# Two layers of a graph transformer on one core: one product per 128 edges for the edge counts, half of the target patterns made as steps by ScalarE, edges loaded first

## The reference, cut to what matters

```
xn  = layernorm(x)
x   = x + gnn(xn, edges) + linear_attention(xn)
x   = x + mixture_of_experts(layernorm(x))        # 16 experts, top 2
```

```
h   = xn @ W + b
adj = zeros(256, 256); adj[src, dst] = 1; adj[dst, src] = 1; adj += eye
adj = adj / row_sum
out = d0 * h + d1 * adj h + d2 * adj^2 h + d3 * adj^3 h ; relu
```

## Time and profile before

| | |
|---|---|
| three runs | 239.66 us median, 238.54 to 239.84 |
| the profiled execution | 238.44 us, its span 236.7 us |
| mean granted clock of TensorE | 0.986 |
| PE busy | 221.0 us, 93% of the span |
| DVE, ACT, POOL busy | 139.3, 51.4, 21.2 us |
| `idle_turns` (133 products recorded in all) | 18.0 us |
| count products, 128 | 14.6 us recorded, 14.0 us of the chain |
| one-hot patterns, 128 | 27.0 us |

### The profile page before, as it was taken

How to read it: one execution, slowest core, us unless ns; L and a number is a source line. 1 busy time by engine, 2 the same in 40 slices (tenths; PEclk the granted TensorE clock), 3 DMA queues, 4 the chain that set the end, 5 groups by cost and what they waited for, 6 DMA issues and landing times.

```text
span 236.7 us, 2953 instructions
## 1 busy us (share of the span) xinstructions
PE 221.0 (93%) x1065; PEld 148.9 (63%) x1065; DVE 139.3 (59%) x432; ACT 51.4 (22%) x118; POOL 21.2 (9%) x36
## 2 busy tenths in 40 slices
PE   0699999999999989999999999999988999989994
PEld 0584647598569866985455668549674454648851
DVE  2796689995488813324062726979771649534312
ACT  2103021132202011211001116971082412014200
POOL 2940100000010200000005000000020001010000
PEclk9999999999999589999999999999999999999999
DMA  6998894001999000004604000000000000000002
GB/s 156 332 404 319 324 415 161 0 3 39 384 408 405 8 0 0 3 0 138 217 33 147 0 1 1 0 3 0 0 0 3 0 0 0 1 0 3 0 0 89
DMA packets 8669, 23.65 MB, mean 100 GB/s; under 512 B 2376, under 2 KB 2376, under 8 KB 8400
## 3 DMA queue, kind: packets, MB, share of 16 engines
q1 hardware_dynamic: 8656, 23.48, 26.9%
HBM read 22.95 MB, written 0.52 MB: 99 GB/s over the span
## 4 chain that ended last, share of the span: by engine, by line
PE 88%; DVE 6%; DMA 1%; POOL 1%; issue 1%; ACT 1%; SPq 0%; DVEq 0%
PE bank L1102 16%; PE bank L1076 13%; PE bank L1194 9%; PE bank L1206 9%; PE bank L1113 7%; PE bank L1151 6%; PE bank L1255 6%; PE bank L1245 3%; PE bank L1157 3%; PE bank L1158 2%; PE bank L1142 2%; PE bank L1090 2%; PE bank L1293 1%; DVE xT L586 1%; DMA xa<-in_x 1%; PE bank L1294 1%
## 5 line engine op out<-in xcount | busy, mean ns | idle before, releaser
L1102 PE MATMUL bank<-raw,xT 128*128 128x512 f32 x88 | 39.1, 594 | 0.0
L773 DVE TENSOR_SCALAR ring<-iota_bf,edges 128x256 bf16<-128x256 bf16 x128 | 27.0, 300 | 5.4 <-PE bank L1255 5.3
L1102 PEld LDWEIGHTS bank<-raw,xT 128*128 128x128 f32 x88 | 16.4, 190 | 18.9 <-issue 18.7
L303 POOL TENSOR_TENSOR rstd<-veps,minus_half 128x1 f32<-128x1 f32 x14 | 8.7, 632 | 170.8 <-DVE veps L573 89.1
L1194 PE MATMUL bank<-xT,raw 128*128 128x256 f32 x96 | 22.7, 386 | 0.0
L1206 PE MATMUL bank<-raw,ring 128*128 128x512 f32 x48 | 21.0, 594 | 0.0
L1194 PEld LDWEIGHTS bank<-xT,raw 128*128 128x128 f32 x96 | 17.6, 190 | 3.1 <-issue 0.9
L1245 PE MATMUL bank<-iota_bf 128*128 128x256 bf16 x133 | 18.0, 295 | 0.3 <-ACT wa L336 0.3
L1113 PE MATMUL bank<-xT,raw 128*128 128x256 f32 x64 | 16.2, 411 | 0.8 <-DVE xT L586 0.8
L1245 PEld LDWEIGHTS bank<-iota_bf 128*128 128x128 bf16 x133 | 14.0, 106 | 4.2 <-issue 1.1
L1206 PEld LDWEIGHTS bank<-raw,ring 128*128 128x128 f32 x48 | 9.0, 190 | 10.9 <-issue 10.5
(11 more groups left out here) (241 smaller groups left out, 323.6 us busy)
## 6 DMA issues: line engine op xcount, KB each, us to landing
raw<-in_up SPq DMA_DIRECT2D x6, 512.0 KB, 9.2
raw<-in_down SPq DMA_DIRECT2D x6, 512.0 KB, 11.0
raw<-in_k SPq DMA_DIRECT2D x4, 512.0 KB, 9.0
raw<-in_q SPq DMA_DIRECT2D x4, 512.0 KB, 9.8
raw<-in_v SPq DMA_DIRECT2D x4, 512.0 KB, 11.3
raw<-in_out SPq DMA_DIRECT2D x4, 512.0 KB, 8.8
raw<-in_gat SPq DMA_DIRECT2D x4, 512.0 KB, 6.7
raw<-in_gnn SPq DMA_DIRECT2D x2, 512.0 KB, 10.2
```

The costliest lines, as they stand in the source:

```text
L303: nc.gpsimd.tensor_tensor(rstd[:, t:t + 1], veps[:, t:t + 1], minus_half[:, t:t + 1], ALU.pow)\
L773: ins = V.tensor_scalar(onehot[:, j % RING, a, :], iota_bf[:, :], edges[:, a, j:j + 1], None, ALU.is_equal)
L1102: ins = mm(bank[banks[t]][:, :], xT_at(c, t), w.at(c), start=c == 0, stop=c == C - 1)
```

## The change

- **Counts.** A source is split in its number modulo 128 and a digit that says whether it is 128 or more. The pattern of sources has 128 columns and holds the value 1, or -4096 where the digit is set (`radix`). One product per `j` of 128 weights by 256 columns gives both halves of the sources in one number: count of the low half minus 4096 times count of the high half. There are 64 products in place of 128.
- **Targets.** For even `j` DVE writes the one-hot pattern of the targets as before. For odd `j` ACT writes `Sign(iota - dst + 0.5)`, a step that is -1 below the target and +1 from it on (line 414). Even `j` are summed in bank 2, odd ones in bank 3; DVE takes the differences of neighbours of half the sum of bank 3, adds up, converts to integers, shifts by 12 bits, and takes the two halves apart: ten instructions more (lines 820 to 837). The result is laid out as `countT`, and PE transposes it into `count`.
- **Pieces.** The ring has 20 slots of 384 values; the counts stand in pieces of 20, 20 and 24, all ahead of gnn0. The gnn0 product is cut in its two tiles, the second behind the context product.
- **Start.** `src` and `dst` are loaded ahead of `x`. DVE's work on `iota` and on the edges stands ahead of the statistics of `x`. PE does 20 `idle_turns` before the first transposes.
- **After.** Parts 0 and 1 of the small products stand behind step 2, parts 2 and 3 behind step 3. The 40 `idle_turns` ahead of the next `xn` are 8. Some banks change, and the queries' transposes go to banks 4 and 5.

```
@@ sync
+            for a, n in enumerate(("src", "dst")):
+                sp.dma_start(edges_i[:, a, :], A[n].rearrange("(p j) -> p j", p=P)).then_inc(edges_in, 16)
             for t in range(T):
                 sp.dma_start(xa[:, t, :], A["x"][t * P:(t + 1) * P, :]).then_inc(x_in, 16)
...
-            load(0, 2)
-            for a, n in enumerate(("src", "dst")):
-                sp.dma_start(edges_i[:, a, :], A[n].rearrange("(p j) -> p j", p=P)).then_inc(edges_in, 16)
-            load(2, 8)
+            load(0, 8)
...
-            sp.wait_ge(count_full, 1)
+            sp.wait_ge(sums_full, 1)
@@ scalar
+            def steps_part(j0, j1):
+
+                for j in range(j0 + 1, j1, 2):
+                    if j >= RING:
+                        act.wait_ge(onehot_used, j - RING + 1)
+                    nc.scalar.activation(onehot[:, j % RING, P:P + N], iota_bf[:, :], ACT.Sign,
+                                         bias=turn[:, j:j + 1]).then_inc(steps_ready, 1)
+
+            act.wait_ge(iota_bf_ready, 1)
+            act.wait_ge(turn_ready, 1)
+            steps_part(0, 8)
             xT_part(0, 0)
+            steps_part(8, 20)
             mix_exps(0)
+            steps_part(20, 40)
             mix_q(0)
+            steps_part(40, 64)
             mix_v(0, (6, 7))
...
@@ vector
+            dve.wait_ge(iota_ready, 1)
+            V.tensor_copy(iota_bf[:, :], iota_i[:, :]).then_inc(iota_bf_ready, 1)
...
+            dve.wait_ge(edges_in, 32)
+            go(V.tensor_copy(edges[:, :, :], edges_i[:, :, :]))
+            settle()
+            go(V.tensor_scalar(radix[:, :], edges[:, 0, :], float(P), None, ALU.is_ge))
+            V.tensor_scalar(turn[:, :], edges[:, 1, :], -1.0, 0.5, ALU.mult, ALU.add).then_inc(turn_ready, 1)
...
             dve.wait_ge(x_in, 16 * T)
...
             def onehots(j0, j1):
                 for j in range(j0, j1):
                     if j >= RING:
                         dve.wait_ge(onehot_used, j - RING + 1)
-                    for a in range(2):
-                        ins = V.tensor_scalar(onehot[:, j % RING, a, :], iota_bf[:, :], edges[:, a, j:j + 1], None,
+                    ins = V.tensor_scalar(onehot[:, j % RING, 0:P], iota_bf[:, 0:P], edges[:, 0, j:j + 1],
+                                          radix[:, j:j + 1], ALU.is_equal, ALU.mult)
+                    if j % 2 == 0:
+                        ins = V.tensor_scalar(onehot[:, j % RING, P:P + N], iota_bf[:, :], edges[:, 1, j:j + 1], None,
                                               ALU.is_equal)
...
+            def counts():
+
+                dve.wait_ge(sums_full, 1)
+                go(V.tensor_copy(sums[:, 0, :], bank[2][:, 0:N]))
+                go(V.tensor_scalar(steps[:, 1:N + 1], bank[3][:, 0:N], 0.5, None, ALU.mult))
+                settle()
...
+                go(V.tensor_tensor(sums[:, 1, :], steps[:, 1:N + 1], steps[:, 0:N], ALU.subtract))
+                settle()
+                go(V.tensor_copy(sums_i, sums))
+                settle()
+                go(V.tensor_scalar(sums_i, sums_i, FIELD_BITS, None, ALU.arith_shift_right))
...
+            hidden_rows(0)
             context(6)
+            hidden_rows(1)
...
@@ tensor
+            pe.wait_ge(iota_bf_ready, 1)
+            idle_turns(1, 20)
             pe.wait_ge(consts, 1)
             xT_made(0, xn, (0, 1))
             k_of("k0", k_full, 0)
...
                     pe.wait_ge(onehot_ready, j + 1)
-                    for t in range(T):
-                        ins = mm(half(COUNTB[t], 0), onehot[:, j % RING, 1, t * P:(t + 1) * P],
-                                 onehot[:, j % RING, 0, :], start=j == 0, stop=j == ET - 1)
+                    if j % 2:
+                        pe.wait_ge(steps_ready, j // 2 + 1)
+                    ins = mm(half(2 + j % 2, 0), onehot[:, j % RING, 0:P], onehot[:, j % RING, P:P + N],
+                             start=j < 2, stop=j >= ET - 2)
...
+            pe.wait_ge(hr_ready, 2)
             pe.wait_ge(yT_ready, 2)
             attn_out("out0", 0).then_inc(o_full, 1)
...
-            idle_turns(5, 40)
+            idle_turns(5, 8)
```

More of the change, by code:

```diff
@@ L122, in gps_two_layers @@
         hr = sb("hr", [P, T, D])
+        sums_i = hr[:, 0, :].bitcast(i32).rearrange("p (g n) -> p g n", g=2)
+        sums = hr[:, 1, :].rearrange("p (g n) -> p g n", g=2)
+        steps = sb("steps", [P, N + 1])
         both_hi = sb("both_hi", [P, 2, T * D], f32r)
@@ L788, in _, with hidden_rows @@
+            counts()
             dve.wait_ge(small_in, SMALLS)
-            for t in range(T):
+            dve.wait_ge(countT_ready, 2)
+            def hidden_rows(t):
                 dve.wait_ge(h_full, t + 1)
                 V.tensor_tensor(hr[:, t, :], bank[t][:, :], row["b_gnn0"], ALU.add).then_inc(hr_ready, 1)
-            onehots(48, 64)
-            dve.wait_ge(b_down_ready, 1)
-            for t in range(T):
-                dve.wait_ge(cur_rounded, t + 1)
-                V.tensor_tensor(cur_lo[:, 0, t, :], hr[:, t, :], cur_hi[:, 0, t, :].bitcast(f32), ALU.subtract)\
-                    .then_inc(cur_ready, 1)
-                go(V.tensor_scalar(diffused[:, t, :], hr[:, t, :], diffusion[:, 0:1], None, ALU.mult))
+            hidden_rows(0)
@@ L799, in _ @@
             context(6)
-            dve.wait_ge(count_ready, 2)
-            go(V.tensor_scalar(far[:, :, :], count[:, :, :], 1.0, None, ALU.min))
+            hidden_rows(1)
+            dve.wait_ge(countT_ready, 2)
+            go(V.tensor_scalar(far[:, :, :], countT[:, :, :], 1.0, None, ALU.min))
             settle()
-            dve.wait_ge(countT_full, 1)
-            go(V.scalar_tensor_tensor(linked[:, :, :], bank[7][:, :].rearrange("p (c n) -> p c n", c=T), 1.0,
+            dve.wait_ge(count_full, 1)
@@ L816, in _ @@
             V.reciprocal(degree[:, :], degree[:, :]).then_inc(degree_ready, 1)
+            dve.wait_ge(b_down_ready, 1)
+            for t in range(T):
+                dve.wait_ge(cur_rounded, t + 1)
+                V.tensor_tensor(cur_lo[:, 0, t, :], hr[:, t, :], cur_hi[:, 0, t, :].bitcast(f32), ALU.subtract)\
+                    .then_inc(cur_ready, 1)
+            for t in range(T):
+                go(V.tensor_scalar(diffused[:, t, :], hr[:, t, :], diffusion[:, 0:1], None, ALU.mult))
             dve.wait_ge(degree_ready, 1)
@@ L1259, in counts @@
                 return ins
-            COUNTB = (2, 3)
+            assert ET // 2 * P <= int(FIELD)
+            counts(0, 20)
             rows_of("q0", (0, 1), q_full, 0)
-            counts(0, 16)
+            counts(20, 40)
             rows_of("v0", (6, 7), v_full, 0)
-            counts(16, 32)
-            pe.wait_ge(q_shifted, 2)
-            rows_of("gnn0", (0, 1), h_full, 0)
-            counts(32, 48)
+            counts(40, 64).then_inc(sums_full, 1)
             pe.wait_ge(ekT_ready, 4)
             ek_made(0, (4, 5))
-            pe.wait_ge(hr_ready, 2)
+            pe.wait_ge(q_shifted, 2)
+            rows_of("gnn0", (0, 1), h_full, 0, (0,))
             pe.wait_ge(q_ready, 2)
-            qT_made((0, 1))
+            pe.wait_ge(ek_ready, 2)
+            qT_made((4, 5))
             pe.wait_ge(v_ready, 2)
-            pe.wait_ge(ek_ready, 2)
             context(6)
-            counts(48, 64).then_inc(count_full, 1)
+            rows_of("gnn0", (0, 1), h_full, 0, (1,))
+            pe.wait_ge(countT_ready, 2)
+            for t in range(T):
+                for s in range(T):
+                    ins = nc.tensor.transpose(bank[3][:, t * N + s * P:t * N + (s + 1) * P],
+                                              countT[:, s, t * P:(t + 1) * P], ident[:, :])
+            ins.then_inc(count_full, 1)
             pe.wait_ge(ctx_ready, 2)
@@ L1280, in _ @@
             yT_made(0, (4, 5))
-            pe.wait_ge(count_ready, 2)
-            for s in range(T):
-                for t in range(T):
-                    ins = nc.tensor.transpose(bank[7][:, s * N + t * P:s * N + (t + 1) * P],
-                                              count[:, t, s * P:(s + 1) * P], ident[:, :])
-            ins.then_inc(countT_full, 1)
             def diffuse(i, banks):
```

77 lines of the change are left out of this document (46 added, 31 removed).

## The result

| | before | after |
|---|---|---|
| four runs, median | 239.1 us (238.37 to 239.84) | 230.49 us (228.31 to 232.56) |
| profiled execution | 238.44 us, span 236.7 | 230.77 us, span 229.1 |
| mean granted clock | 0.986 | 0.968 |

Ratios leave out executions over 1.5% above the fastest of their kernel (here the one of 232.56), medians and ranges take in all. The ratio is 0.961, 95% interval 0.955 to 0.967: faster by 8.6 us in the medians and by 7.7 us between the two profiles. Forecast were 230.0 us in a range of 225 to 235, and 8.9 us between profiles. The time came out where it was said. Of the six terms of its sum four came out at their size or within their bounds; the other two, the start (off by 2.5 us) and the debt of the low clock (off by 2.2), lay outside their bounds, in opposite directions, and one effect, at the very end, was not in it.

The account below looks back on a forecast made before the run. PE, busy for 93% of the span, was taken as the bound. Counts -7.0, attn_out wait +0.4, start -0.3, small products 0, turns -5.0, clock debt +3.0 sum to -8.9: 229.5 us profiled, 230.0 forecast, range 225.0 to 235.0.

Parts of the forecast that it names:

- the start: Up to k0: edge loads delay x by 0.94 us, 20 turns win back 1.2; net -0.3 us (-1.9 to +1.4).
- debt of the low clock: Transposes of xn, gate's product and first `up` products run at half speed behind only 8 turns: +3.0 us (1.5 to 6).
- counts: Count products on PE: 64 instead of 128 at 0.109 us each, 7.0 us instead of 14.0: -7.0 us.
- wait at `attn_out`: PE waits longer between yT and `attn_out`, as ACT rounds the second `hr` tile first: +0.4 us (0 to 0.8).
- Feeding them: Patterns for the count products: narrow DVE pattern 0.16 us (0.07 to 0.25), ACT's step 0.4 to 0.49; cost nothing.
- Taking apart: Ten DVE instructions separating the counts behind the last count product: 4.9 us (3.5 to 7.5), hidden beside PE, cost nothing.
- Thin products: Small products behind the third diffusion step: thin stretch 5.1 to 6.8 us, clock falls; net 0 (-1.0 to +0.7).
- All goes well: Rival: warm k0, clock back by the gate, no wait at yT, thin stretch ends early; 225.5 us, chance 0.14.
- Clock stays low long: Rival: PE enters the experts at 1.2 GHz, recovers after 6 us or more, k0 cold; 234 us, chance 0.14.
- DVE in the middle: Rival: taking apart at 7.5 us and patterns at 0.25 make countT 2 to 4 us late; 232.5 us, chance 0.09.
- Slow pattern: Rival: two-factor pattern makes PE wait from 0.27 us, spends the gain from 0.41; 241.2 us at 0.45, chance 0.05.
- Edges hold up x by more: Rival: starting turns or edges' issue delay x by more than 0.94 us; gain of 7 left, no own chance.

Follow-up runs that it names:

- experiment 7: The changed kernel with 36 idle turns at the start in place of 20; 231.0 us (228.25 to 232.61).
- experiment 11: The changed kernel with x loaded first, edge work behind the copies of xT, 26 starting turns and two turns after each thin piece; 230.66 us, median of six.
- experiment 12: The changed kernel with the edges' loads issued by ACT instead of SP and 30 turns at the start; 230.43 us (228.28 to 233.13).
- experiment 4: The changed kernel without the 20 idle turns at the start; 231.86 us (229.37 to 233.16), ratio 0.968.
- experiment 2: The changed kernel with 40 idle turns instead of 8 ahead of xn's transposes; 235.72 us (233.87 to 237.53).
- experiment 3: The changed kernel with every count product issued twice, so the counts come out doubled; 237.64 us (235.38 to 239.81).
- experiment 8: The changed kernel with every 128-column pattern written once more to a buffer nothing reads; 245.95 us (244.72 to 247.02), ratio 1.030.
- experiment 9: The changed kernel with the 128-column pattern as a plain one-factor comparison, which gives wrong counts; one run, 232.47 us.
- experiment 5: The changed kernel with x loaded before the edges, DVE's edge work behind `norm_rows`, ACT's steps behind its copy of xT; 234.57 us (232.22 to 234.98).
- experiment 6: The changed kernel with x loaded first and the edge work behind the copies of xT on DVE and ACT; 230.48 us (228.68 to 231.73).
- experiment 10: The changed kernel with two idle turns after each piece of the thin products, 15 in all instead of 8; 233.01 us (232.46 to 235.19).
- experiment 1: The kernel before the change with 8 idle turns instead of 40 ahead of the next xn; 238.2 us (234.74 to 238.6).

## Why the prediction came out right

Differences between the two profiles, all read from the chains:

| term | forecast | measured |
|---|---|---|
| counts | -7.0 | -7.0 |
| wait at `attn_out` | +0.4 | +0.5 |
| start, to k0's end | -0.3 | +2.2 |
| between counts and turns, else | 0 | -1.0 |
| turns | -5.0 | -4.9 |
| debt of the low clock | +3.0 | +0.8 |
| last `down` products | 0 | +1.7 |
| sum | -8.9 | -7.7 |

*Counts.* 64 products in 6.98 us, 0.109 each, none waited for; issuing them twice put back 7.0 us of the chain (7.15 in the medians). Their waits cost nothing, the lower end of the bound.

*Feeding them.* The narrow pattern is 0.225, not 0.16, inside 0.07 to 0.25; ACT's steps come every 0.41, at the low end of 0.4 to 0.49. Cost nothing, as said, but k0 was long. The prediction's threshold (PE waits from 0.27) was not tested, since no run has a price between 0.225 and 0.45, and it left out where the room is short, in the first piece: with k0 at the full level experiments 7, 11 and 12 wait there at 0.225.

*Taking apart* took 4.2 us (4.9 said). *The wait at `attn_out`* is the 0.73 us of issue against 0.6 said; the rest of the +0.5 is the count transposes (0.44), now ahead of yT.

*Start: the step that failed most.* Forecast -0.3 with bounds -1.9 to +1.4 (its own terms, 0.94 less up to 2.3, reach only -1.4); measured +2.2, outside both. 1.0 of it is k0's later start, 1.2 its length. x landed at 5.82 us, 1.7 later instead of 0.94: its own transfer took 3.65 instead of 2.92. In eight kernels with the edges ahead on SP's queue it landed at 5.02, 5.09, 5.17, 5.20, 5.30, 5.82, 7.08 and 7.11 us, in the kernels with x first at 4.03 to 4.22. So 0.94 was right for the usual run, and the profile of after (and two others) caught a later one, which a bound from the issues' price alone did not hold. The larger miss is the credit of the 20 turns: 1.2 us to be gained, where k0 lost 1.19 and the transposes won 0.63 (1.31 us, against 1.94 without turns). The level rose between the last turn (6.1 us) and the transposes (8.8), as hoped, but it was lost at 9.7, behind a pause of 2.7 us, and came back only at 16.5. So the credit rested on two things that do not hold each time: with 20 turns the level rose ahead of k0 in four of eight kernels (experiment 4) and was held through k0 in none, 8.5 us or more; with 26 to 36 turns and pauses up to 1.3 us it was held in all three (experiment 7). There k0 took 7.14 us and the transposes 1.12, so a held level is worth 1.6 and 0.8 us against the 8.74 and 1.94 of a start without turns; the 0.45 that the prediction gave the transposes was too little, the 1.87 for k0 about right. That k0 took longer than in the earlier trace rows need not be the turns' doing, since it did so without them (10.10); in the kernels with 0 or 20 turns there it took 8.5 to 10.1 us, by nothing that I changed on purpose. Of the Trainium skill's two rules named there, that sustained activity releases the throttle agrees with the rise in after (1.31 us for 1.94). That transposes do not count could not be told: in experiment 7 they stood between turns and k0, 1.12 us long, and k0 ran at the full level.

*Thin products* took 5.27 us for 24 (48 records), inside 5.1 to 6.8, and the clock held longer than before, until 74.6. In the other variants they took 5.3 to 6.8. With the 0.2 us of the context product that is nearly all of the row "else" of the table. No run undoes the new places of the small products or of gnn0's second tile alone, so that they cost nothing is read from the chain, not shown by a run.

*Debt: the other step that failed.* +0.8 with what follows the transposes, instead of +3.0 and under its bounds (1.5 to 6). The mechanism is there, but it has two sizes: the gate's product took 1.89 us in the profiles of after and of experiments 2, 3, 4, 8, 9 and 12, and 3.57 in those of experiments 5, 6, 7, 10 and 11, with a debt of about 3 in all. +3.0 was one of the two; what selects between them I did not find. It goes by neither the number of turns nor the place of the transposes: these stood at 76.8 us in after and at 77.0 in experiment 11.

*The end.* In the profile of after and in those of all twelve experiments the last `down` products take 8.77 or 8.78 us, only in the profile of before 7.08. The prediction held that all that happens up to xn's transposes passes to the end one for one. It does not quite: the same products met another clock. Why is open. The time alone doesn't tell, since before's start at 226.5 us and the others' at 216.7 to 232.3, and experiment 1, which differs from before in the turns alone, has the 8.78.

So the misses of start (+2.5) and debt (-2.2) cancelled, and of the end's +1.7 the thin products and context gave 1.0 back. The time is right to 0.5 us by more luck than the terms deserve; the range of 225 to 235 held it with room.

*The rivals.* "All goes well" fell by the k0 at the low level; two of its four parts came true, the clock's return by the gate's product and 0.8 us of the 1.0 in the thin products. "Clock stays low long" did not happen in after, whose level was back by 78 us [stretch 78 to 79 above]. "DVE in the middle" did not occur; ek's transposes follow the last count directly. "Slow pattern" did not occur; experiment 8, made at its price, is slower than before, as it says, by 6.4 us in the medians. "Edges hold up x by more" happened in part: 1.67 us instead of 0.94, and in two other profiles 2.9 and 3.0.

Of what the prediction said would show: x landing (5.1, was 5.82), `attn_out` (52.4, was 54.85, with 0.73 idle), the transposes of xn (75, was 76.8) are late mostly by the start's 2.5 us; the clock was back by 80, as said; k0 at 9.93 is neither of the two values named.

Open are why x lands 2 us later still in some runs with the edges ahead, what selects the long or the short low stretch, what lost the level ahead of k0, and why the last products of before alone ran at the full level.

## What to carry to other kernels

Halve the products on the bound engine first: that was the largest term, it was kept in full (7.0 of 7.0), and doubling the products gave it back. Idle turns have no fixed price: cutting 32 of them was worth 0.5 us in one kernel and 4 to 5 in the next, so read the granted clock of the products behind them before their removal is counted as gain. When a warm start is bought, look at which engine feeds the next product: in experiment 7 k0 ended 3.6 us earlier than in after, of which DVE's patterns took 0.8, slower thin products 0.6 and the low clock behind them, 55 us later, 1.9.

## What had not been expected of the hardware

- Small DVE instructions beside POOL's `MEMSET` and the instruction behind it: 0.20 us alone, 1.79 and 1.88 beside them, each starting just behind POOL's and ending about when it does (9.67 against 9.61, 11.84 against 11.79). The first narrow patterns of after, too, took 1.1 us apiece beside POOL's work, against 0.22. The Trainium skill, page "SBUF — State Buffer" (Who interferes with whom), says that such a DVE instruction and one of GpSimd share a pair of ports, that whoever issues first has it for the whole instruction, and that the other is blocked until it ends. The rows agree.
- A pattern with two per-partition factors costs 0.225 us for 128 bf16 columns, with one 0.162, and one of 256 columns 0.195: the second factor weighs more than 128 more columns.
- Products with 2 columns did not hold the clock, although PE is busy for 100% of the stretch: 2.00 us busy of 2.00 at 0.71 granted, in experiment 12 (at 0.50 in the two microseconds behind it):

```profile
70.00:72.00 2.00, 2.00 (x15) 2.00 (x14) 2.00 (x5) 0.00 (x0) 0.00 (x0) 0.71 0.00 0
```
